# One row of maxima or two: score banks in fixed pairs, and an auxiliary ring of two PSUM banks

## The reference, cut to what matters

```python
x = x + tanh(g_xattn) * cross_attention(layernorm(x), ctx)        # 16 heads of 64, 1444 context rows
x = x + tanh(g_ffn) * block(layernorm(x))                         # self-attention, 8 experts, top 2
# cross_attention, for each of the 16 batch entries:
sim = einsum('bhid,bhjd->bhij', q, k) * 64 ** -0.5                # 16 heads x 100 tokens = 1600 rows
attn = softmax(sim, axis=-1)
out = einsum('bhij,bhjd->bhid', attn, v)
```

## Time and profile before

| | us |
|---|---|
| median of 3 runs | 1325.35 (1325.32 to 1327.8) |
| the profiled execution, its own time | 1323.73 |
| its span, first to last instruction | 1322.0 |
| PE busy | 1249.3 (95%) |
| DVE busy | 935.8 (71%) |
| ACT busy | 824.1 (62%) |
| POOL busy | 767.5 (58%) |
| mean granted TensorE clock | 0.984 |

### The profile page before, as it was taken

One profiled execution on the slowest core, in us unless ns is written; L12 is line 12 of the kernel. 1 busy time (PEld: TensorE's weight loads), 2 busy tenths in 40 slices (PEclk: granted clock), 3 DMA queues, 4 the chain that ended last, 5 costly groups with the idle time before them and its releaser, 6 DMA issues.

```text
span 1322.0 us, 34615 instructions
## 1 busy us (share of the span) xinstructions
PE 1249.3 (95%) x14472; PEld 911.7 (69%) x14472; DVE 935.8 (71%) x1714; ACT 824.1 (62%) x1476; POOL 767.5 (58%) x603
## 2 busy tenths in 40 slices
PE   6789999999999999999999999999999999789998
PEld 5356777777677777777776767677777776567776
DVE  5697776768675868685858676767767685956676
ACT  1345666667666766666666666666666666555654
POOL 3144666565656566665656565756565646654554
PEclk9798999999999999999999999999999999999999
DMA  6201503030313030302020302111021300000000
GB/s 172 65 1 34 167 14 80 14 80 14 81 13 81 13 80 14 80 10 77 13 74 15 78 16 55 40 41 53 18 75 14 63 14 15 14 15 1 8 8 14
DMA packets 122278, 57.28 MB, mean 43 GB/s; under 512 B 108262, under 2 KB 117706, under 8 KB 122122
## 3 DMA queue, kind: packets, MB, share of 16 engines
q1 hardware_dynamic: 122122, 55.07, 17.5%
HBM read 15.38 MB, written 0.82 MB: 12 GB/s over the span
## 4 chain that ended last, share of the span: by engine, by line
PE 73%; DVE 13%; ACT 10%; issue 3%; DMA 1%; SPq 0%; DVEq 0%; ACTq 0%
PE psum L777 17%; PE psum L758 9%; PE psum L858 8%; PE psum L759 8%; PE psum L760 8%; PE psum L793 5%; PE psum L890 3%; PE psum L912 3%; PE psum L903 3%; PE psum L805 3%; DVE mx L1309 3%; DVE p_lo L449 2%; DVE kbd L1329 2%; ACT p L985 2%; ACT p_hi L991 2%
## 5 line engine op out<-in xcount | busy, mean ns | idle before, releaser
L449 POOL TENSOR_TENSOR p_lo<-p,p_hi 128x768 f16<-128x768 f32 (+1 forms) x192 | 349.6, 1827 | 256.0 <-ACT p_hi L986 163.3
L1309 DVE TENSOR_REDUCE mx<-psum 128x1 f32<-128x512 f32 (+1 forms) x585 | 360.8, 651 | 38.5 <-PE psum L858 32.9
L985 ACT ACTIVATE p<-psum 128x768 f32<-128x768 f32 (+1 forms) x256 | 215.0, 840 | 243.6 <-PE psum L760 243.4
L777 PEld LDWEIGHTS psum<-c_both,p_hi 128*128 128x128 f16 x4992 | 255.2, 98 | 61.7 <-issue 30.3
L777 PE MATMUL psum<-c_both,p_hi 128*128 128x97 f16 (+1 forms) x4992 | 281.2, 207 | 2.1 <-ACT acc_sb L1001 1.1
L758 PE MATMUL psum<-qk_hi,cT_both 97*128 97x384 f16 (+1 forms) x768 | 259.6, 338 | 17.2 <-ACT p_hi L991 9.1
L759 PE MATMUL psum<-qk_lo,cT_both 96*128 96x384 f16 (+1 forms) x768 | 258.4, 336 | 0.0
L760 PE MATMUL psum<-qk_hi,cT_both 96*128 96x384 f16 (+1 forms) x768 | 256.3, 334 | 0.0
L858 PE MATMUL psum<-cT_both,qk_hi 96*128 96x512 f16 (+1 forms) x585 | 215.9, 369 | 10.9 <-DVE kbd L1329 4.9
L449 DVE TENSOR_TENSOR p_lo<-p,p_hi 128x768 f16<-128x768 f32 (+1 forms) x192 | 205.0, 1068 | 16.7 <-ACT p_hi L986 15.3
L990 ACT ACTIVATE p<-psum 128x384 f32<-128x384 f32 (+1 forms) x256 | 130.0, 508 | 135.5 <-PE psum L760 135.5
(11 more groups left out here) (201 smaller groups left out, 2115.7 us busy)
## 6 DMA issues: line engine op xcount, KB each, us to landing
c_both<-c_new SPq DMA_DIRECT2D x16, 768.0 KB, 3.5
ctx_nat<-in_ctx_dram SPq DMA_DIRECT2D x16, 528.0 KB
aT<-a_new SPq DMA_TRANSPOSE x64, 2.9
wg<-in_L_ffn_e_gate_dram SPq DMA_DIRECT2D x1, 1024.0 KB, 5.5
wu<-in_L_ffn_e_up_dram SPq DMA_DIRECT2D x1, 1024.0 KB, 7.8
wd<-in_L_ffn_e_down_dram SPq DMA_DIRECT2D x8, 128.0 KB, 4.9
out_dram<-x SPq DMA_DIRECT2D x4, 200.0 KB
x<-in_x_dram SPq DMA_DIRECT2D x1, 600.0 KB
```

The costliest lines, as they stand in the source:

```text
L449: engine.tensor_tensor(p_lo[0:m, i % 3, 0:w], p32[0:m, i % 3, 0:w], p_hi[0:m, i % 3, 0:w], ALU.subtract).then_inc(lo_made(b, i)[0], 1)
L777: t = mm(psum[:, ACCB + bank, k * (C + 1):k * (C + 1) + wide], p[0:m, i % 3, n * P:(n + 1) * P], c[parity][0:m, j, 0:wide], start=(j == 0 ...
L985: a(to32, src, ACT.Exp, scale=DH ** -0.5)
L1309: v.tensor_reduce(mx[:, rt, part:part + 1], bank[:, 0:w], AX.X, ALU.max)\
```

## The change

It splits the row of maxima in two. Group 0 (tiles 0 to 5) and group 1 (tiles 6 to 12) get an mrow tile, a transposing step ("m" and "m1") and a semaphore each. The steps p of batch b+1's group 0, and of its tiles 6 and 7, stay in batch b (24 steps, units 10 to 23). The other 15 become steps "o", made in units 0 to 8 of the batch that they are for; m1 stands in unit 10, and unit 12 waits for its DMAs. Before batch 0 only 8 of the 13 steps w are left. The scores take banks 0 to 3 in two fixed pairs, the accumulators banks 4 and 5, and the auxiliary ring has the two banks 6 and 7. ACT always takes both halves in one instruction. The layer norm steps of batch 0 move from units 7 to 15 to units 0 to 10.

```diff
+    NP0 = TILES[0] * MP
+    AHEAD = NP0 + 2 * MP
-    share = {i: 0 for i in range(3, 21)}
+    for i, n in spread(range(AHEAD, NPU), range(10)):
+        plan[i].append(("o", n))
+    for i, n in spread(range(NP0), range(10, 21)) + spread(range(NP0, AHEAD), range(21, UNITS)):
+        plan[i].append(("p", n))
+    plan[10].append(("m1", 0))
+    plan[21].insert(0, ("m", 0))
...
-           [("w", n) for n in range(3, 6)] + [("q", 3)] + [("w", n) for n in range(6, RT)] + [("m", 0)]
+           [("m", 0), ("q", 3)] + [("w", n) for n in range(6, AHEAD // MP)]
...
-        ACCB, AUXB, DOWNB = 3, 5, 4
-        SCORE_BANKS = ((0, 1), (0, 2), (1, 2))
-        FIRST_FREE = ((0, 1), (1, 0), (0, 1))
+        ACCB, AUXB, DOWNB = 4, 6, 4
+        SCORE_BANKS = ((0, 1), (2, 3))
...
-                ring, bank = (2, 1 + k % 2) if kind in ("prep", "end") else (3, (base[0] + k) % 3)
+                ring, bank = 2, (base[0] + k) % 2
...
+            def send_second_row(b, parity, free):
+                sp.wait_ge(aux_free, free + 1)
+                sp.dma_start(qk_hi[parity][C:C + 1, ROW0[1]:(RT - 1) * P], mrow[1][0:TILES[1] - 1, :]).then_inc(row2_in, 16)
                 sp.dma_start(qk_hi[parity][C:C + 1, (RT - 1) * P:ROWS],
+                             mrow[1][TILES[1] - 1:TILES[1], 0:rows_of(RT - 1)]).then_inc(row2_in, 16)
...
                 if i == 0:
-                    pe.wait_ge(row_in, (b + 1) * 32)
+                    pe.wait_ge(row_in, (b + 1) * 16)
+                    if isinstance(b, int) and b == 0:
+                        pe.wait_ge(wide_free, AHEAD // MP)
+                if i == CH:
+                    pe.wait_ge(row2_in, (b + 1) * 32)
...
-                for n, k in enumerate(FIRST_FREE[i % 3]):
-                    if n:
+                for k in range(2):
+                    if k:
                         halfway()
-                    if n and (b or i):
-                        pe.wait_ge(probs_hi, b * UNITS + i)
```

More of the change, by code:

```diff
@@ L85, in flamingo_kernel, with spread @@
         load[i] += 0 if i - 1 in LO_POOL else .9
-    share = {i: 0 for i in range(3, 21)}
[L87 to L96, removed]
+    NP0 = TILES[0] * MP
+    AHEAD = NP0 + 2 * MP
+    def spread(maxima, units):
+        counts = {i: 0 for i in units}
+        for _ in maxima:
+            i = min(counts, key=lambda i: (load[i], i))
+            counts[i] += 1
+            load[i] += .6
+        left = iter(maxima)
+        return [(i, next(left)) for i in units for _ in range(counts[i])]
+    for i, n in spread(range(AHEAD, NPU), range(10)):
[4 more added lines that the diff above has]
+    plan[21].insert(0, ("m", 0))
     ROUTER = ["max", "sub", "sum", "inv", "prob", "best0", "tie0", "rank0", "first0", "pick0", "drop",
@@ L118, in flamingo_kernel @@
         plan[13 + n].append(("x1", n))
[L119 to L120 removed]
+    PREP = [("q", 0), ("q", 1)] + [("w", n) for n in range(3)] + [("q", 2)] + [("w", n) for n in range(3, 6)] + \
+           [("m", 0), ("q", 3)] + [("w", n) for n in range(6, AHEAD // MP)]
     NE = 4 * EU
@@ L160, in one_maxima_first @@
     def one_maxima_first(units):
-        maxima = [u for u in units if u[0] == "p"]
+        maxima = [u for u in units if u[0] in ("p", "o")]
         if sum(u[0] not in NO_BANK for u in units) < 3 or not maxima:
@@ L260, in flamingo_kernel @@
         mneg = sb("mneg", [P, RT], F16)
-        mrow = sb("mrow", [RT, P], F16)
+        mrow = [sb(f"mrow{r}", [TILES[r], P], F16) for r in range(2)]
         n1 = sb("n1", [D, 1])
@@ L551, in _ @@
             turn(B - 2, 1)
+            second_row_of(B - 1, "last", 1)
             turn(B - 1, 0)
@@ L673, in body @@
                 for i in range(UNITS):
-                    if kind == "first" and i in (9, 11, 13):
-                        token_rstd((i - 7) // 2)
+                    if kind == "first" and i in RSTD_UNITS:
+                        token_rstd(RSTD_UNITS.index(i) + 1)
                     if i == CTX_LO_AT and b + 2 < B:
@@ L980, in probs @@
                     act.wait_ge(pv, b * UNITS + (i - 2))
-                first, second = SCORE_BANKS[i % 3]
+                first = SCORE_BANKS[i % 2][0]
                 to32, to_hi = (t[0:m, i % 3, 0:2 * w].rearrange("p (k w) -> p k w", k=2) for t in (p32, p_hi))
[L983 to L991, removed]
+                src = psum[0:m, first:first + 2, 0:w]
+                a(to32, src, ACT.Exp, scale=DH ** -0.5)
+                ins = a(to_hi, src, ACT.Exp, scale=DH ** -0.5)
                 ins.then_inc(probs_hi, 1)
@@ L1065, in body @@
                 for i in range(UNITS):
-                    if kind == "first" and i == 0:
+                    if kind == "first" and i == 3:
                         ctx_hi_parts(1, kind, 1)
```

90 lines of the change are left out of this document (54 added, 36 removed).

## The result

The changed kernel takes 1339.41 us (median of 4 runs, 1337.91 to 1341.74) against 1325.34 for the kernel before (median of 4 beside it): ratio 1.0114, 95% interval 1.0098 to 1.0129. It is slower by 1.1%, where I had forecast 1321 and faster. The profiled execution took 1340.15, its span is 1338.3, and the mean granted clock is 0.984 as before.

The account below looks back on a forecast made before the run. PE's instruction stream bounds middle batches, DVE stretches at both ends. Opening -8.8, batch 0 -4, 14 middle batches +7.0 and batch 15 +1.5 sum to -4.3 on a 1322.0 span: 1317.7, forecast 1321 us against the runs, range 1305 to 1333.

Parts of the forecast that it names:

- the walk through unit 4: Middle batch, unit 4: waits of 0.42 us, reckoned with p_lo at 0.9.
- The opening: Before batch 0: fewer reductions let unit 0 start at 42.3 instead of 51.08, -8.8 us.
- What goes in a middle batch: Middle batch: waits for exponentials and accumulators gone, those of units 4, 5 and 10 replaced; together -3.0 us.
- Units 0 to 5: Middle batch: q ahead of p_lo and a maxima step, with two ring banks, adds waits of +1.55 us.
- twice 1.55: Middle batch, units 0 to 5: upper bound on the added waits, if each unit hands its delay on.
- Units 8, 10 and 12: Middle batch: new waits of 0.16 us for o35, +1.24 for kbd's bank, and +0.28 for the second row's DMA.
- Batch 0: First batch: DVE's work unchanged at 62.95 us plus 13 of idle time makes 76, -4 (bounds 0 and -8).
- Batch 15: Last batch: +2 for maxima in units 0 to 8, -1.4 for bank waits gone; together +1.5 us (-2 to +6).
- (b): Units 0 to 5 and 10: the ring of two costs more; at 1.2 a middle batch, 1331 us; chance 0.21.
- (d): Both ends: only the opening gains, batch 0 gives 0 and batch 15 +5, so 1328 us; chance 0.12.
- (a): Units 0 to 5: no convoy of delays forms, a middle batch at -1.05, 1299 us in all; chance 0.15.
- (c): Unit 12: the second row is late, a wait of 1.0 instead of 0.28, +10, 1331 us; chance 0.07.

Follow-up runs that it names:

- the last run: Kernel before, with the maxima in units 4 to 20 instead of 3 to 20, so q3 stands alone behind its p_lo: 1334.0 us, ratio 1.006.

## Why the prediction was wrong

The span was to come out at 1317.7 and is 1338.3. Of the 20.6 between them, 10.4 stand in batch 0 and 9.4 in batches 1 to 14. Two steps failed: the walk through unit 4 took a duration of p_lo that no longer held, and the sum for batch 0 put the ring of two at nothing and DVE's work at what it was.

**The opening: right.** Unit 0 starts at 42.45 (forecast 42.3), and two reductions behind q3 end there, as worked out. The DMA is hidden.

**What goes in a middle batch: right.** The waits of 0.36, 0.17, 0.55 and 0.4 are gone.

**Units 0 to 5: the step that failed.** I walked these units "with these durations", p_lo at 0.9 from the earlier trace rows, "0.42 in unit 4". The waits measured up to unit 3 add to 0.43 (0.11 and 0.05 in unit 1, 0.06 in unit 2, 0.21 in unit 3), where the walk had 0.53, and unit 5 waits 0.61 for 0.60. Only unit 4 is off, 1.13 for 0.42: p_lo takes 1.65 there, since in the new order it falls behind an operation of GpSimd. That is 0.7 in each of 14 batches, 10 us, and the run with that work cut short gives back 10.4 in those batches and leaves a wait of 0.09. I took a duration from a row whose surroundings the change altered. My bound "twice 1.55" was wide enough, but for another reason ("if each unit hands its delay on").

**Units 8, 10 and 12: right.** The waits are 0.16, 1.25 and 0.22, for 0.16, 1.24 and 0.28.

**Batch 0: wrong by 10.4.** "I take 13 of idle time, so 76": 62.95 of DVE's work and 13 of idle time. Measured were 67.20 and 19.1. The work grew by 4.3. That is in the main p_lo beside GpSimd: four of them, which take 0.94 to 1.01 alone, take 2.34 in unit 3, 1.85 and 1.96 in unit 15 and 2.57 in unit 17, and in batch 0 of the kernel before none took more than 1.02. With the old banks three of the four are there too, so this part comes with the order. Of the idle time, 7.7 goes with the banks, since it is 11.5 with the old ones. I costed the ring of two at nothing there, though with two banks every wait of DVE for PE and of PE for DVE comes sooner: PE waits 3.3 in unit 4 for a bank whose maximum stands behind layer norm work in DVE's queue, and 2.8 in unit 17 for one whose maximum stands behind 1.23 of that work and the p_lo of 2.57. With the ring of three neither wait is there (the longest are 2.5 in unit 3 and 2.7 in unit 8), but in unit 17 p_lo is also at 1.02 there, so the ring and the long p_lo are not told apart in that unit. With the old banks batch 0 takes 77.85, near the forecast.

**Batch 15: right in its sum by luck.** +2.1 for +1.5. I had +2 for units 0 to 9; against 28.62 in the earlier trace rows they took:

```profile
1111.54:1150.02 38.48, 29.09 (x320) 21.74 (x319) 32.16 (x47) 17.17 (x25) 18.65 (x14) 0.87 0.07 13
```

That is +9.9, and units 10 to 17 with -4.5, units 18 to 22 with -0.9 and all behind with -2.3 took most of it back. The greatest part of the +9.9 stands behind one operation of VectorE beside a row of GpSimd's, with the longest wait of PE in the whole changed kernel:

```profile
1137.01 7.17 DVE L1180 SCALAR_TENSOR_TENSOR wg_lo<-wg,n,wg_hi 128x768 f16<-128x768 f32 x1
1137.73 3.23 POOL L459 TENSOR_TENSOR p_lo<-p,p_hi 128x768 f16<-128x768 f32 x2
1140.92 2.45 POOL L687 TENSOR_TENSOR cT_both<-h2T,c_both 128x1200 f16<-128x1200 f32 x1
...
1144.74 0.43 PE L924 MATMUL psum<-ident,hn 100*128 100x100 f32 x1 [7.48 <-DVE mx L1336]
```

wg_lo, a part of the expert weights' split, takes 1.01 in other units. Here it lasts through all of these GpSimd operations and ends 0.81 after the last of them (1144.18 after 1143.37), and the maximum that PE needs stands behind it. It takes 7.16 to 7.17 in all eleven profiles with two rows, with either set of banks, and 2.38 to 2.39 in all three with one row. So it comes with the two rows, not with the banks. No run took that GpSimd work away, so that GpSimd is the cause is argued from these rows and not shown. The runs of the parts give +5.1 for the two rows and -5.9 for the banks; I had +2.9 and -1.4. The parts add to -0.8, so some of it belongs to neither alone. The -5.9 is -2.8 in units 0 to 9, -0.8 and -0.9 in the next two stretches and -1.3 behind; what makes it so large was not tried.

**The rivals.** (b) named the sign and nearly the price (1.1 for a middle batch where it said 1.2) and the place, units 0 to 5. Its cause, the ring of two, is only part: against the old banks the changed kernel's middle batch is 0.8 longer, of which unit 10 alone has 0.7, and the wait for p_lo in unit 4 is there with three banks as well. As a time, its 1331 is 8 short: it kept my -4 for batch 0. (d) erred to the same side as I did in batch 0. (a) and (c) did not come.

## What to carry to other kernels

When a change moves an instruction, its duration moves with it: look at what will then run beside it on the other engines, above all GpSimd beside VectorE, and walk with the longer duration where the two meet. Put what PE waits for next ahead of what it needs later: the order of one q and one maximum in each of units 0 to 3 was worth 21.5 us here, and m1 one unit earlier 12; but q3 moved alone in the kernel before cost 0.6%, since p_lo then met GpSimd. Split a change of several parts before judging it: the banks alone cost 1.4%, the two rows alone nothing, and on the old banks, with two small edits of the order, the two rows gain 2.1%.

## What the runs showed of the hardware

**DVE and GpSimd hold each other up for whole operations.** p_lo of 128x768 takes 0.94 alone. In unit 4 it takes 1.65 in the changed kernel and 1.86 in the one with q behind p_lo, and ends 0.81 after a GpSimd operation in both cases (633.09 after 632.28, 617.78 after 616.97): it is not slower but late. wg_lo in batch 15 also ends 0.81 after the GpSimd operation that it outlasts. The other way round, p_lo keeps its 0.94 and GpSimd is late: its first product ends 1.17 after the end of p_lo both in unit 3 of the changed kernel (631.01 after 629.84) and in the last run (630.36 after 629.19), nearly its own 1.31.

Which of the two is late can't be read from the starts of the rows. Of these cases of p_lo, GpSimd's row began first in each: by 0.47 and 0.26 where p_lo was late, by 0.40 and 0.24 where GpSimd was, and by 0.06 in the earlier trace rows, where GpSimd was late too.

The Trainium skill, SBUF — State Buffer, in SBUF: two separate sides, says that a VectorE operation with two SBUF inputs and a GpSimd operation that reads SBUF share one pair of ports, which the one that starts first holds for its whole length. By that rule unit 4's p_lo would have ended 0.94 after 632.28, and the wait would be 0.93 instead of 0.80: the trace agrees within 0.13. On who holds the ports the rows above don't bear the rule out, if a row's start is taken for the operation's.

**A long wait of PE is paid twice.** In batch 0 of the changed kernel PE stands still for the 3.16 us before 63.14, and in the next 5.31 the granted clock is 0.50, its lower level of 1.2 GHz:

```profile
59.98:63.14 3.16, 0.00 (x1) 0.00 (x1) 3.06 (x5) 0.06 (x1) 1.64 (x1) 0.89 1.23 277
63.14:68.45 5.31, 5.31 (x32) 3.54 (x32) 5.11 (x9) 1.51 (x2) 1.23 (x2) 0.50 0.29 122
```

Score matmuls start 0.32 apart in that stretch instead of 0.16. The clock is 0.50 in two later stretches of this batch as well, 76.12 to 82.94 and 110.25 to 113.66, and PE stood still for 1.60 before 74.76 and for 2.62 before 109.56. In the whole of batch 0 PE's busy time is 3.4 longer than before (73.54 for 70.16) at a clock of 0.86 for 0.91. Not all of that is due to these waits: the clock was also at 0.50 from 35.16, ahead of unit 0, to 48.81.
